# LSTM then GRU on one core: the second group of x moved to another DMA queue and read a tick later

## The reference

```python
# x (32, 128, 512), cond (32, 512): B = 32 sequences, T = 128 steps, D = 512
xW = einsum('ntd,dg->ntg', x, Wx) + b            # LSTM, h0 = cond, c0 = 0
a = xW[t] + h @ Wh                               # i, f, o, g: 4 x 512
c = f * c + i * g;  h = o * tanh(c)              # sigmoid / tanh gates
x = x + hs                                       # residual
z = sigmoid(x @ W_z + g @ U_z + cond @ C_z + b_z)   # GRU over the new x, g0 = 0
r = sigmoid(x @ W_r + g @ U_r + cond @ C_r + b_r)
hh = tanh(x @ W + (r * g) @ U + cond @ C + b)
g = (1 - z) * g + z * hh
out = x + gs
```

## Time and profile before

| | |
|---|---|
| median of 3 runs | 1211.89 us (1211.66 to 1212.92) |
| the profiled execution's own time | 1213.73 us |
| its span | 1211.9 us |
| busy: PE, DVE, ACT, POOL | 97%, 82%, 38%, 29% |
| chain that ended last, by engine | PE 87%, DVE 4%, SP's queue 3%, issue 2%, DMA 1% |
| HBM | 30.93 MB read, 8.39 MB written |

### The profile page before, as it was taken

One profiled execution on the slowest core, in us unless ns is written; L12 is line 12 of the kernel. 1 busy time (PEld: TensorE's weight loads), 2 busy tenths in 40 slices (PEclk: granted clock), 3 DMA queues, 4 the chain that ended last, 5 costly groups with the idle time before them and its releaser, 6 DMA issues.

```text
span 1211.9 us, 76123 instructions
## 1 busy us (share of the span) xinstructions
PE 1174.7 (97%) x34774; PEld 868.1 (72%) x34774; DVE 995.2 (82%) x2922; ACT 464.9 (38%) x1119; POOL 346.8 (29%) x628
## 2 busy tenths in 40 slices
PE   5899999999999999999999999999999999999997
PEld 1467675566777777777777787787777778777775
DVE  2769788887888888888888888888888888888876
ACT  5565334443333333333333333333333333333332
POOL 3100244423223223232332323233232322323221
PEclk9899999999999999999999999999999999999999
DMA  9901311100111100111110011111011111101001
GB/s 312 324 11 21 142 21 21 21 8 17 22 21 21 22 12 13 22 21 22 21 22 9 17 22 22 22 21 22 6 19 22 22 22 21 21 7 19 13 13 20
DMA packets 142674, 44.21 MB, mean 36 GB/s; under 512 B 135888, under 2 KB 136144, under 8 KB 140816
## 3 DMA queue, kind: packets, MB, share of 16 engines
q1 hardware_dynamic: 140656, 38.68, 13.4%
q0 software_dynamic: 640, 0.53, 0.2%
q10 hardware_dynamic: 1056, 0.13, 0.1%
HBM read 30.93 MB, written 8.39 MB: 32 GB/s over the span
## 4 chain that ended last, share of the span: by engine, by line
PE 87%; DVE 4%; SPq 3%; issue 2%; DMA 1%; ACT 1%; POOL 1%; DVEq 0%; POOLq 0%
PE ps_g L986 37%; PE ps_l L986 28%; PE ps_l L1049 16%; PE ps_g L995 3%; PE ps_c L1049 3%; SPq L298 2%; DMA o_area<-in_L_cond_C_dram 1%; PE ps_l L995 1%; SPq L302 1%; DVE zr L671 0%; DVE gates L671 0%; POOL stage L384 0%; ACT zr L577 0%; DVE rgT L908 0%; DVE rg L906 0%
## 5 line engine op out<-in xcount | busy, mean ns | idle before, releaser
L986 PE MATMUL ps_l<-wh,h2T 128*32 128x512 f16 x5952 | 344.8, 379 | 0.0
L986 PE MATMUL ps_g<-w,y2T 128*32 128x384 f16 x5760 | 256.4, 326 | 1.8 <-issue 1.8
L986 PEld LDWEIGHTS ps_l<-wh,h2T 128*32 128x32 f16 x5952 | 156.1, 97 | 133.2 <-issue 1.2
L423 POOL TENSOR_TENSOR yT<-xT,hT 128x128 f32<-128x128 f32 x128 | 62.0, 485 | 566.3 <-DVE hT L841 566.3
L986 PEld LDWEIGHTS ps_g<-w,y2T 128*32 128x32 f16 x5760 | 158.8, 97 | 90.2 <-issue 2.2
L986 PE MATMUL ps_g<-u,g2T 128*32 128x256 f16 x5760 | 179.4, 273 | 0.0
L986 PEld LDWEIGHTS ps_g<-u,g2T 128*32 128x32 f16 x5760 | 155.7, 97 | 15.1
L671 DVE SCALAR_TENSOR_TENSOR zr<-ps_g,sc,term 128x256 f32<-128x256 f32 x128 | 61.8, 483 | 81.5 <-PE ps_g L986 77.8
L376 POOL TENSOR_TENSOR o_area<-yT,gT 128x128 f32<-128x128 f32 x127 | 58.8, 463 | 203.6 <-DVE gT L967 202.7
L986 PE MATMUL ps_g<-u,rg2T 128*32 128x128 f16 x5760 | 102.7, 219 | 9.6 <-DVE rg2T L665 8.8
L986 PEld LDWEIGHTS ps_g<-u,rg2T 128*32 128x32 f16 x5760 | 86.7, 96 | 20.2 <-DVE rg2T L665 14.2
(11 more groups left out here) (128 smaller groups left out, 1855.3 us busy)
## 6 DMA issues: line engine op xcount, KB each, us to landing
x_nat<-in_x_dram SPq DMA_DIRECT2D x126, 64.0 KB, 2.6
out_dram<-o_area SPq DMA_DIRECT2D x124, 64.0 KB, 1.9
wh<-in_L_cond_Wx_dram SPq DMA_DIRECT2D x4, 1024.0 KB, 11.3
stage<-in_L_cond_Wx_dram SPq DMA_DIRECT2D x4, 1024.0 KB, 9.1
w<-in_L_cond_Wh_dram SPq DMA_DIRECT2D x3, 1024.0 KB, 19.4
u<-in_L_cond_Wh_dram SPq DMA_DIRECT2D x1, 1024.0 KB, 25.0
stage<-in_L_cond_W_z_dram SPq DMA_DIRECT2D x1, 1024.0 KB, 8.5
stage<-in_L_cond_W_r_dram SPq DMA_DIRECT2D x1, 1024.0 KB, 8.2
```

The lines of the kernel that those rows point to most:

```text
L423: nc.gpsimd.tensor_tensor(yT[:, q, :], xT[:, r, P * q:P * q + P], hT[:, n % 2, :], ALU.add).then_inc(yT_done, 1)
L986: mm = nc.tensor.matmul(bank[B * j:B * j + B, c0:c1].rearrange("p (n c) -> p n c", c=B), still(a, k), moving(b, k, j), start=opens and (a, ...
```

## The change

Three parts. (1) SP's `load(Q, 1)` is gone. ACT issues the same four transfers in tick 0, after the tanh of LSTM step 0 and before the squares of Wh chunks 2 and 3. (2) POOL waits for Wh chunk 0 to land before it issues the sixteen bias transfers. (3) DVE's `largest(1)` moves from tick 0 to tick 1, where it stands ahead of `turn(1)` and behind `common(0, 0)`; `lstm_scales(1, 1)` moves from tick 1 to tick 2; PE's `bound(1, 1)` moves from tick 1 to tick 2.

```diff
@@ sync
                 sp.dma_start(wh_raw[k], wh[P * k:P * k + P, :]).then_inc(wh_in[k], 16)
-            load(Q, 1)
             for g, w in enumerate((w_z, w_r, w_h)):
@@ gpsimd
+            pool.wait_ge(wh_in[0], 16)
             for j in range(J):
                 pool.dma_start(term0[rows(j), :, :].rearrange("b g (k p) -> b (g k) p", k=K),
@@ scalar, after_state
                 if t == 0:
+                    for j in range(J):
+                        act.dma_start(x_nat[rows(j), 1, :].rearrange("b (n p) -> b n p", p=B), natural(x, Q)[j]).then_inc(x_in[1], 16)
                     wh_squared(2)
                     wh_squared(3)
@@ vector, after_state
                     wx_low(2)
-                    dve.wait_ge(x_in[1], 16 * J)
-                    largest(1)
                 if t == T_WH:
                     common(0, 0)
+                    dve.wait_ge(x_in[1], 16 * J)
+                    largest(1)
                     turn(1)
-                    lstm_scales(1, 1)
                     dve.wait_ge(wx_hi, 3)
                     wx_low(3)
...
+                if t == T_WH + 1:
+                    lstm_scales(1, 1)
```

More of the change, by code:

```diff
@@ L747, in after_state @@
                     wx_low(2)
+                if t == T_WH:
+                    common(0, 0)
                     dve.wait_ge(x_in[1], 16 * J)
                     largest(1)
-                if t == T_WH:
-                    common(0, 0)
                     turn(1)
-                    lstm_scales(1, 1)
                     dve.wait_ge(wx_hi, 3)
```

## The result

The changed kernel took 1219.25 us (median of 6 executions, 1218.41 to 1221.23), the kernel before beside it 1211.78 us (6, 1211.17 to 1213.36). The ratio is 1.0061 with an interval of 1.0050 to 1.0072: 7.5 us, or 0.6%, slower. 1216.7 was forecast. The two profiled executions lie only 4.9 us apart: 1213.73 and 1218.64 us, spans of 1211.9 and 1216.8.

A forecast was written before the change was run, and what follows sets the result against it. PE was taken as the bound, 87% of the chain, with the change an early shift carried along: 1211.9 + 4.4 (PE) + 0.4 (scales) = 1216.7 us; own range 1213.5 to 1220, eight in ten 1211.0 to 1220.0.

The forecast's parts named there:

- x at 50.0: x group 1 on ACT's queue, taking turns with weight packets, lands at 50.0 us; bounds 48.5 and 51.5.
- Biases, a gain of 0.4: POOL's bias transfers start after Wh chunk 0, most still beside Wh; Wh gains 0.4 us, bounds 0 and 1.7.
- ACT's issues, nothing under the cover of the wait: ACT's four x issues take 4 x 0.5 us; covered by the wait to 50.0, no cost, otherwise 0.5.
- DVE +4.6: Tick 1: DVE waits for x until 50.0, so wx_low(3) starts at 51.4 instead of 46.80.
- PE +4.4: GRU step 1: g at 62.7, 64 products at the lower clock take 3.9 us; z and r start at 66.6, not 62.18.
- The scales, +0.4: lstm_scales in tick 2 starts ACT 1.6 us later, gates of tick 3 1.1 later; 0.7 hidden, 0.4 us left.
- The sum, 4.8: Whole kernel: +4.4 for PE and +0.4 for the scales, a shift for both profiled execution and median.
- x in time: Rival: x lands before 45 us; -1.4 to +0.4 us, time 1211.4, no change that can be told; chance 0.2.
- faster: Rival: biases out of Wx's and Wh's way, x in time, PE's clock high: -3.1, 1208.8 us; chance 0.1.
- the gain of the C stream can't reach the end: Rival rejected: after C, PE waits for g from DVE, whose chain has only 2.1 us of slack; no chance given.
- The marks: Signs expected in the changed profile: C 2 to 4 us earlier, named DVE, PE and ACT idle stretches, 4.8 us later from tick 4.
- No long SP issues with a hole behind them: Sign in the changed profile: SP has no long issues followed by a hole in transfers at 28 to 32 us.

The follow-up runs named there:

- wide pieces: Changed kernel with x group 1 on ACT's queue in pieces of 512 bytes instead of 128, columns permuted: 1209.11 against 1211.87 us before, ratio 0.9974.
- later read: Changed kernel with DVE's wait for x, reduction and transpose moved behind the low parts of tick 1: 1212.43 against 1213.46 us before, ratio 0.9996.
- busy PE: Changed kernel plus 125 small unread products on PE in tick 2, ahead of its wait for g: 1216.70 against 1211.87 us before, ratio 1.0041.
- this part alone: Kernel before with only POOL's wait for Wh chunk 0 ahead of the biases: 1211.19 against 1211.97 us, ratio 0.9993.
- versions with x on SP: Changed kernel with x group 1 on SP's queue: behind W, ratio 1.0001 (scales in tick 1: 0.9990); behind C, read later, 0.9990 (PE kept busy: 0.9977).

## Why the prediction was right, and where it was off

**Direction and mechanism: right.** The queues took turns one for one (704 to 705), x came last, DVE stood in front of `largest`, PE in front of g, and its 64 passes ran at the lower clock. The wide pieces, the later read and the busy PE each took away their own link of that chain, and the time went with it.

**x at 50.0: it was 51.3.** Errors both ways. ACT's issues began at 33.44 instead of 35.1, since Wh came 1.7 us sooner, not 0.4, and the first did not wait for the end of the tanh. The turns took 12.0 us, at 91 ns for 95. But 5.8 us went around them instead of 2.4: the first piece moved at 37.1, 3.7 us behind the first issue, and x landed 2.1 us behind the point where 132 turns from there would end (49.15). By 49.5 all but 14 of the 2112 pieces were through; these are the lagging engines, for which "some tenths" had been put.

**Biases, a gain of 0.4: mis-sized.** The text had most of them still go beside Wh. Wh was 1.7 us sooner (1.5 in the run of this part alone), at the upper bound. In the forecast's own range the sum of the lower bounds, 1.5 + 1.8 + 1.3 us below 1216.7, is 1212.1 and not 1213.5.

**ACT's issues, nothing under the cover of the wait: right in the changed kernel**, but the term was too small. The four took 3.6 us, not 2.0, and PE waited 1.83 us for the squares of Wh, which took away all that the biases had given: DVE came to x at 45.16, where before it was at 45.38.

**DVE +4.6 was +5.8, PE +4.4 was +5.4.** The 1.3 us of x, carried on. The low level had 3.64 us for the 64 passes against 3.9 forecast, and did not reach the r * g product (1.08 us), as counted.

**The scales, +0.4: was 0 in tick 3.** ACT's wait came as worked out (1.71 us), but PE's product of tick 3 is 5.37 us late as that of tick 2 is. The 0.7 us that were counted as hidden hid all of it. The 0.7 us that go at step 15 in the kernels with the scales in tick 2 were not foreseen.

**The sum, 4.8, against 7.5 measured.** The step that failed is "as a shift the sum holds for both". The profiled pair moved by 4.9, the medians by 7.5. That 4.9 is so near to 4.8 is luck in part: DVE and PE were 1.0 us later than counted, the scales 0.4 less, and the gap of 5.4 us at step 1 had come down to 4.9 at the end. The profiles lie on different sides of their medians, in before twice on the high side. The executions of the changed kernel fall in two groups: three of 1218.4 to 1218.6 us with a mean clock of 0.992 to 0.994, three of 1219.9 to 1221.2 us with 0.989 to 0.990. A lower mean clock says that in this half PE stood longer at the low level than in the profiled one. That the range was gone with the busy PE (within 1 us) fits; that it is this idle stretch that makes both groups is not shown, and no execution of the slower group was profiled.

**Rivals.** "x in time" was forecast as -1.4 to +0.4. The run with wide pieces made it real, and gave -2.8: nearer to the "faster" rival of -3.1, whose gain from the biases it also had. That the gain of the C stream can't reach the end held for the changed kernel, where PE had g to wait for. In the versions with x on SP, C is on the chain again, and with C at 46.17 z and r come 4.4 us before, more than the 2.1 us of slack that the forecast gave DVE's chain.

**The marks.** C landed 3.5 us sooner, DVE, PE and ACT stood as named, and the 64 passes took 57 ns each. "No long SP issues with a hole behind them" held only in its second half. SP stood 5.86 and 11.66 us in the issues of W_r and W, too, but in 28 to 32 us the DMA engines moved 347 GB/s instead of 132 and 41, since what stood in the queue was 2 KB packets and not x.

## What to carry to other kernels

A transfer in small pieces costs little while the other queues are idle and a great deal beside a busy one: count its pieces for each engine and multiply by the time of one packet of the other queue. Here 132 pieces waited for 132 weight packets, 12 us for 256 KB. If such a transfer can't be made coarser, put it behind the last transfer that the chain waits for, and put the engine's wait for it behind work that doesn't need it; the same late x cost 7.5 us ahead of DVE's weight work, and behind it nothing that the times can tell.

## What the runs showed of the hardware

- Two queues with work on the same engines got equal numbers of packets, 704 of 128 bytes beside 705 of 2 KB; of the time, 14.9% against 95.1%. The Trainium skill ("DMA: Bandwidth & Descriptors", section on queues, rings and completion order) has the engine switch after a whole packet of some 9 to 17 descriptors. Equal counts fit turns of one as well as equal turns of many. The start of the trace of before speaks for turns of one. From 4.7 to 7.1 us, beside 8 KB packets of some 0.34 us each, ACT's queue had its last 11 pieces of x done one at a time, where a drained batch of nine would take 0.13 us at 14 ns a piece.
- An issue can hold its engine for long when much is queued ahead of it. Four x transfers took SP 9.7 to 11.2 us behind queued weights (20.8 in before), against 0.5 us each at the start. ACT's four took 3.6 us while SP's queue had weights, and 1.8 us with a quarter of the pieces. In both the first piece moved 3.6 to 3.7 us behind the first issue.
- Behind 7.9 us without work PE's granted clock was 0.50; with 6.8 us of small products in that stretch the same 64 passes took 1.95 us instead of 3.64.
